# Batch 0's queries, keys and parts inside the self-attention pairs, and pair 7's norm inside the first maxima

## The reference

```
x = layernorm(x + self_attention(x))        # 4 heads, learned windows, q = (x Wq) Wqkv
x = layernorm(x + cross_attention(x, ctx))  # 16 heads of 16 channels
x = layernorm(x + experts(x))               # 8 experts, 2 per token
# cross attention:
Q = x wq + bq;  K = ctx wk + bk;  V = ctx wv + bv
out = softmax(Q K / 4) V, then @ wo + bo
```

## Time and profile before

| | |
|---|---|
| median of 3 runs | 664.44 us (661.35 to 665.6) |
| profiled execution | 663.6 us, its span 661.5 us |
| PE busy | 622.6 us (94%) |
| DVE busy | 373.1 us (56%) |
| ACT busy | 315.1 us (48%) |
| POOL busy | 292.3 us (44%) |

### The profile page before, as it was taken

One profiled execution on the slowest core, in us unless ns is written; L12 is line 12 of the kernel. 1 busy time (PEld: TensorE's weight loads), 2 busy tenths in 40 slices (PEclk: granted clock), 3 DMA queues, 4 the chain that ended last, 5 costly groups with the idle time before them and its releaser, 6 DMA issues.

```text
span 661.5 us, 16872 instructions
## 1 busy us (share of the span) xinstructions
PE 622.6 (94%) x5901; PEld 531.3 (80%) x5902; DVE 373.1 (56%) x996; ACT 315.1 (48%) x813; POOL 292.3 (44%) x526
## 2 busy tenths in 40 slices
PE   6999977999999998999999989999999999999994
PEld 5999954677777776777667768899999999999994
DVE  1778786777777876778767867322222222222245
ACT  2455452777777766777667676121121222112124
POOL 5245365334363349443773342424343342425244
PEclk9999996999999998999989999999999999999998
DMA  8232204565666644444443348688676777666443
GB/s 269 84 93 75 64 28 129 155 193 179 204 191 192 196 135 106 125 119 114 120 107 93 99 140 297 221 274 224 202 211 226 231 231 220 211 195 204 179 138 139
DMA packets 72897, 109.36 MB, mean 165 GB/s; under 512 B 9786, under 2 KB 50562, under 8 KB 72066
## 3 DMA queue, kind: packets, MB, share of 16 engines
q1 hardware_dynamic: 66882, 100.40, 48.7%
q0 software_dynamic: 5952, 8.14, 5.4%
HBM read 73.77 MB, written 12.44 MB: 130 GB/s over the span
## 4 chain that ended last, share of the span: by engine, by line
PE 50%; DMA 19%; issue 10%; DVE 7%; POOLq 6%; POOL 6%; ACT 2%; SPq 0%; DVEq 0%; ACTq 0%
DMA accd<-y,si 18%; PE ps L1603 7%; PE ps L1655 6%; PE ps L1677 6%; PE ps L1630 5%; POOLq L725 5%; PE ps L1614 5%; PE ps L1535 3%; PE ps L1698 2%; PE ps L1663 2%; PE ps L1524 2%; PE ps L1543 2%; PE ps L804 1%; PE ps L1580 1%; POOL r_ln L365 1%
## 5 line engine op out<-in xcount | busy, mean ns | idle before, releaser
L2160 DVE TENSOR_REDUCE cmx<-ps 100x1 f32<-100x361 f32 x256 | 134.6, 531 | 62.9 <-PE ps L1603 58.7
L804 PE MATMUL ps<-xsT,W 128*128 128x128 f32 x1408 | 164.5, 276 | 0.0
L804 PEld LDWEIGHTS ps<-xsT,W 128*128 128x128 f32 x1408 | 160.6, 192 | 0.3
L1930 ACT ACTIVATE cpr<-ps 128x300 f32<-128x300 f32 x256 | 104.8, 419 | 58.2 <-PE ps L1614 57.7
L1603 PE MATMUL ps<-st 96*100 96x361 bf16 x256 | 86.5, 341 | 5.7 <-DVE cmx L2160 4.5
L1614 PEld LDWEIGHTS ps<-st 120*128 120x128 bf16 x768 | 63.2, 102 | 31.9 <-issue 9.3
L853 PE MATMUL ps<-WD,hT 128*128 x384 | 88.1, 380 | 0.5 <-issue 0.5
L1614 PE MATMUL ps<-st 120*128 120x100 bf16 x768 | 77.2, 209 | 3.6 <-ACT st L1935 1.6
L853 PEld LDWEIGHTS ps<-WD,hT 128*128 128x128 f32 x384 | 70.7, 191 | 8.8 <-issue 0.5
L1008 DVE TENSOR_SCALAR y<-ps,wt 128x256 f32<-128x256 f32 x28 | 13.5, 484 | 106.3 <-PE ps L853 106.3
L719 POOL DMA_INDIRECT accd<-y,si x28 | 44.9, 1605 | 64.2 <-DMA accd<-y,si 55.9
(11 more groups left out here) (267 smaller groups left out, 1026.8 us busy)
## 6 DMA issues: line engine op xcount, KB each, us to landing
W<-in_wgu SPq DMA_DIRECT2D x32, 1408.0 KB, 6.5
st<-parts SPq DMA_DIRECT2D x192, 115.2 KB, 2.5
WD<-in_wd SPq DMA_DIRECT2D x6, 1024.0 KB, 5.6
cx<-in_ctxT SPq DMA_DIRECT2D x16, 361.0 KB, 4.5
x_sb<-in_x SPq DMA_DIRECT2D x8, 200.0 KB
x1d<-x SPq DMA_DIRECT2D x8, 200.0 KB
x1Td<-x1T SPq DMA_DIRECT2D x8, 200.0 KB, 3.3
x1T_sb<-x1Td SPq DMA_DIRECT2D x16, 100.0 KB, 3.5
```

Source lines behind the costliest of these rows:

```text
L804: mm = pe.matmul(out[:, i * P:(i + 1) * P], self.columns(t, k, c), self.xsT[:, t.par, k, :], start=(k == 0), stop=(k == KC - 1))
L1930: act.activation(pr[:, h % (2 * HG), :], ps[:, B_T + h % 2, 0:NCH * L], ACT.Exp).then_inc(exp_ok, 1)
L2160: dve.tensor_reduce(mx[:, half, hh:hh + 1], ps[0:L, B_S + h % 2, 0:CTX], AX_X, ALU.max).then_inc(max_ok, 1)
```

## The change

Batch 0's `queries` move to pair 3 and its `keys` to pairs 4 and 5, all in bank 0, the bank of `q_in`; `q_in` of the next pair waits until ScalarE has copied them out. So that x1T_sb is there, `load_x1T(0)` and `(1)` are issued in SyncE's turn g = 2 and no longer in g = 4. Batch 0's parts are made in pairs 4 to 7: `cast` is ScalarE's version of `first_part`, `rest` and `third_part` stand around the masks on VectorE, `copy_first` ahead of `add_bias` on POOL, and the two `stack` calls in SyncE's turns 6 and 7. Batch 1's keys and queries follow pair 7's scores in turn 7, its first parts are casts on ScalarE too. The turnings of pair 7 have nothing in between any more. VectorE runs pair 7's softmax right behind pair 6's norm, and `a_normalise(7)` moves into the turn i = -1, behind maximum 5; `turn_x1` of pairs 6 and 7 go to heads 6 and 12 of that turn. ScalarE computes `window_out(g)` ahead of the second exponential in all pairs from 1 on. Nothing is computed that wasn't.

```diff
+def keys_bank(b, m):
+    return M0 + m if b else B_QIN
 with nc.Block() as block:
...
             load_x(g + 2)
+        if g == PAIRS - 1:
+            stack(0, 1)
         if 2 <= g < PAIRS:
             store_T(g - 2)
-        if g == 4:
+        if g == 2:
             sp.wait_ge(x1T_out[0], 16)
...
             load_x1T(1)
-        if g == PAIRS - 1:
+        if g == PAIRS - 2:
             stack(0, 0)
-            stack(0, 1)
         if 1 <= g < PAIRS:
...
     load_x1T(2)
-    store_T(PAIRS - 2)
     for i in ITER[1:]:
...
             a_store(PAIRS - 1)
+            store_T(PAIRS - 2)
             store_T(PAIRS - 1)
...
     for g in range(1, PAIRS):
+        if PAIRS - 3 <= g < PAIRS - 1:
+            copy_first(0, g - PAIRS + 3)
         add_bias(g)
...
             finish(g - 1)
-    copy_first(0, 0)
     finish(PAIRS - 2)
-    copy_first(0, 1)
     pool.wait_ge(cross_in, 16 * cross.LOADS)
     pool.tensor_copy(bvr[:, :, :], bv_sb[:, :].unsqueeze(2).to_broadcast([P, KC, L])).then_inc(c_step, 1)
+    copy_first(1, 0)
+    copy_first(1, 1)
     finish(PAIRS - 1)
...
             R.below(pool, GROUP_AT[i])
-        if kq:
+        if kq and i >= 0:
             copy_first(i + 2, 0)
...
         wait(pe, dx_ev, g)
+        if g == PAIRS - 4:
+            pe.wait_ge(q_ev, 1)
+        if g > PAIRS - 4:
+            pe.wait_ge(k_ev, min(g - PAIRS + 4, 2))
         for m in range(KC):
...
         for k in range(KC):
-            mm = pe.matmul(ps[:, M0 + m, 0:CTX], wk_sb[:, k, m * P:(m + 1) * P], cx[b % NX][:, k, :],
+            mm = pe.matmul(ps[:, keys_bank(b, m), 0:CTX], wk_sb[:, k, m * P:(m + 1) * P], cx[b % NX][:, k, :],
                            start=(k == 0), stop=(k == KC - 1))
...
             for k in range(KC):
-                mm = pe.matmul(ps[:, M2, m * L:(m + 1) * L], wq_sb[:, k, m * P:(m + 1) * P],
+                mm = pe.matmul(ps[:, M2 if b else B_QIN, m * L:(m + 1) * L], wq_sb[:, k, m * P:(m + 1) * P],
                                x1T_sb[b % 2][:, k, :], start=(k == 0), stop=(k == KC - 1))
...
             pe.wait_ge(consts, 7)
-        if g == PAIRS:
-            pe.wait_ge(k_ev, 1)
-            keys(1, 0)
-        if 1 <= g <= PAIRS:
-            turn_probs(g - 1, 0)
-        if g == PAIRS - 1:
+        if PAIRS - 5 <= g < PAIRS - 2:
+            pe.wait_ge(dx_ev, g + 1)
+        if g == PAIRS - 5:
             pe.wait_ge(cross_in, 16 * cross.LOADS)
-            pe.wait_ge(dx_ev, PAIRS)
+            queries(0)
+        if g == PAIRS - 4:
             keys(0, 0)
-        if g == PAIRS:
-            pe.wait_ge(q_ev, 1)
-            queries(1)
+        if g == PAIRS - 3:
+            keys(0, 1)
         if 1 <= g <= PAIRS:
+            turn_probs(g - 1, 0)
             turn_probs(g - 1, 1)
-        if g == PAIRS:
-            pe.wait_ge(k_ev, 2)
-            keys(1, 1)
         if g + 1 < PAIRS:
...
         if g == PAIRS - 1:
-            pe.wait_ge(qk_ev, 2 * PAIRS)
-            queries(0)
-            keys(0, 1)
-        if 2 <= g <= PAIRS:
+            pe.wait_ge(dx_ev, PAIRS)
+            keys(1, 0)
+        if 2 <= g < PAIRS:
             turn_x1(g - 2)
+        if g == PAIRS - 1:
+            pe.wait_ge(qk_ev, 2 * PAIRS)
+            queries(1)
+            keys(1, 1)
     for i in ITER[1:-1]:
...
                 query_scores(i + 1, h)
-            if h == 8 and i < 0:
+            if h == 6 and i < 0:
+                turn_x1(PAIRS - 2)
+            if h == 12 and i < 0:
                 turn_x1(PAIRS - 1)
...
+    def cast(b, m):
+        act.wait_ge(k_ev, 2 * b + m + 1)
+        act.wait_ge(q_ev, b + 1)
+        wait(act, kq_in[m], 16 * SLOTS * b)
+        act.activation(parts[:, m, 4, :], kf[:, m, :], ACT.Copy).then_inc(k1_ok, 1)
     def second_part(b, m):
...
         qk_out(g, 1)
-        if g == PAIRS - 1:
+        if g >= 1:
             window_out(g)
...
             weff_out()
-        if g < PAIRS - 1:
+        if g == 0:
             window_out(g)
...
             v_out(g)
+        if g == PAIRS - 5:
+            act.wait_ge(cross_in, 16 * cross.LOADS)
+            act.mul(bq4[:, :], bqk_sb[:, 0:KC], 1.0 / np.sqrt(DH)).then_inc(act_set, 1)
+            act.wait_ge(act_set, 2)
+            queries_out(0)
+        if PAIRS - 4 <= g < PAIRS - 2:
+            keys_out(0, g - PAIRS + 4)
         if g >= 1:
...
             relu(g + 1)
+        if PAIRS - 3 <= g < PAIRS - 1:
+            second_part(0, g - PAIRS + 3)
+        if PAIRS - 4 <= g < PAIRS - 2:
+            cast(0, g - PAIRS + 4)
         if 2 <= g < PAIRS - 1:
             x1T_copy(g - 2)
-    act.wait_ge(cross_in, 16 * cross.LOADS)
-    act.mul(bq4[:, :], bqk_sb[:, 0:KC], 1.0 / np.sqrt(DH)).then_inc(act_set, 1)
-    keys_out(0, 0)
-    act.wait_ge(act_set, 2)
-    queries_out(0)
-    keys_out(0, 1)
-    second_part(0, 0)
+    keys_out(1, 0)
     x1T_copy(PAIRS - 3)
     a_exps(PAIRS - 1, 0)
-    second_part(0, 1)
-    keys_out(1, 0)
+    queries_out(1)
     a_exps(PAIRS - 1, 1)
     probs_out(PAIRS - 1, 0)
-    queries_out(1)
-    probs_out(PAIRS - 1, 1)
     keys_out(1, 1)
-    x1T_copy(PAIRS - 2)
+    probs_out(PAIRS - 1, 1)
+    cast(1, 0)
+    cast(1, 1)
+    second_part(1, 0)
+    second_part(1, 1)
     for i in ITER[1:-1]:
...
                 keys_out(i + 2, 1)
-            if h == 10 and i < 0:
-                x1T_copy(PAIRS - 1)
-            if h == 5 and kq:
+            if h in (7, 13) and i < 0:
+                x1T_copy(PAIRS - 2 if h == 7 else PAIRS - 1)
+            if h == 5 and kq and t:
                 second_part(i + 2, 0)
...
             dve.wait_ge(consts, 7)
+        if PAIRS - 3 <= g < PAIRS - 1:
+            rest(0, g - PAIRS + 3)
+        if g == PAIRS - 1:
+            third_part(0, 1)
         masks(g)
+        if g == PAIRS - 2:
+            third_part(0, 0)
         if g >= 1:
             a_normalise(g - 1)
-    first_part(0, 0)
-    rest(0, 0)
-    softmax_in(PAIRS - 1, (0,))
-    first_part(0, 1)
-    rest(0, 1)
-    third_part(0, 0)
-    softmax_in(PAIRS - 1, (1,))
-    third_part(0, 1)
-    a_normalise(PAIRS - 1)
+        if g == PAIRS - 1:
+            softmax_in(g)
     for i in ITER[1:]:
...
                     R.spread_total(dve)
-            if h == 2 and kq:
+            if h < 2 and i < 0:
+                rest(1, h)
+            if 3 <= h < 5 and i < 0:
+                third_part(1, h - 3)
+            if h == 5 and i < 0:
+                a_normalise(PAIRS - 1)
+            if h == 2 and kq and i >= 0:
                 first_part(i + 2, 0)
-            if h == 3 and kq:
+            if h == 3 and kq and i >= 0:
                 rest(i + 2, 0)
```

More of the change, by code:

```diff
@@ L1741, in _ @@
                         pe.wait_ge(consts, 7)
-                    if g == PAIRS:
-                        pe.wait_ge(k_ev, 1)
-                        keys(1, 0)
+                    if PAIRS - 5 <= g < PAIRS - 2:
+                        pe.wait_ge(dx_ev, g + 1)
+                    if g == PAIRS - 5:
+                        pe.wait_ge(cross_in, 16 * cross.LOADS)
+                        queries(0)
+                    if g == PAIRS - 4:
+                        keys(0, 0)
+                    if g == PAIRS - 3:
+                        keys(0, 1)
                     if 1 <= g <= PAIRS:
                         turn_probs(g - 1, 0)
-                    if g == PAIRS - 1:
-                        pe.wait_ge(cross_in, 16 * cross.LOADS)
-                        pe.wait_ge(dx_ev, PAIRS)
-                        keys(0, 0)
-                    if g == PAIRS:
-                        pe.wait_ge(q_ev, 1)
-                        queries(1)
-                    if 1 <= g <= PAIRS:
                         turn_probs(g - 1, 1)
-                    if g == PAIRS:
-                        pe.wait_ge(k_ev, 2)
-                        keys(1, 1)
                     if g + 1 < PAIRS:
@@ L2056, in _ @@
                             attended_out(i - 1)
-                        if h == 9 and kq:
+                        if h == 9 and kq and t:
                             second_part(i + 2, 1)
@@ L2134, in masks, with softmax_in @@
                     mk.then_inc(mask_ok, 1)
-                def softmax_in(g, halves=(0, 1)):
-                    for hp in halves:
+                def softmax_in(g):
+                    for hp in range(2):
                         n = 2 * g + hp
@@ L2303, in _ @@
                             normalise(i - 1)
-                        if h == 6 and kq:
+                        if h == 6 and kq and i >= 0:
                             third_part(i + 2, 0)
-                        if h == 7 and kq:
+                        if h == 7 and kq and i >= 0:
                             first_part(i + 2, 1)
-                        if h == 8 and kq:
+                        if h == 8 and kq and i >= 0:
                             rest(i + 2, 1)
@@ L2313, in _ @@
                             moments(i - 1)
-                        if h == 11 and kq:
```

(1 more changed line is left out.)

8 lines of the change are left out of this document (4 added, 4 removed).

## The result

The changed kernel takes 669.03 us (median of 18 runs, 665.81 to 672.72), the kernel before 664.66 beside it (18 runs, 661.01 to 666.93). The ratio on record is 1.0075 with a 95% interval of [1.0057, 1.0094]: slower, by 4.4 us in the medians (whose quotient is 1.0066) and by 5.0 us by the ratio. The forecast was 670.3.

The account below looks back on a forecast made before the run. TensorE was taken to bound the pairs, with VectorE's chain in the seam. Moved matmuls 3.5, stall 4.8 and half clock 2.3 us, less 4.3 from the seam, gave 6.3 us later: 670.3 us, range 665 to 674.

Parts of the forecast that it names:

- The moved matmuls: Pairs 3 to 5: batch 0's queries and keys lengthen a TensorE without idle time by 3.5 us.
- The wait: Pair 3: TensorE stalls 4.8 us (bounds 1.5 to 5.8) until x1T_sb is stored and loaded back.
- The half clock behind it: After pair 3's stall: 4 to 6 us at half clock, costing 2.3 us (0 to 3.8).
- Sum at pair 7: At pair 7's start: moved matmuls, stall and half clock together make it 10.6 us later.
- Pairs 6 and 7 fit: Pairs 6 and 7: the parts fit into VectorE's idle time at zero cost, pairs again taking 10.1 us.
- The seam: Pair 7's start to first key scores: +36.7 us (35.3 to 38.5) instead of +41.05, giving back 4.3 us.
- To the end, one for one: Batches behind the seam: TensorE is saturated, so a shift at the first key scores passes nearly whole to the end.
- The stall is absent: Rival, pair 3: data is there when TensorE comes, 0.8 us less than before, 662.8 us; chance 0.06.
- Short transfers: Rival, pair 3: store and load take 2.0 us each, stall 1.5 us, 664.3 to 666.6 us; chance 0.08.
- The seam returns little: Rival, seam: half clock for all 16 heads' scores, return only 1.8 us, time 672.5 us; chance 0.14.
- The stall without the clock: Rival, pair 3: the stall comes but the clock holds, 2.3 us less, 668 us; chance 0.10.
- Faster: Rival: no stall, and the first maximum's 9 us gain survives as the norm fits into waits; 658 us, chance 0.04.

Follow-up runs that it names:

- nowait: Changed kernel with batch 0's queries reading a tensor present from the start, so without the wait for x1T_sb; 664.24 us, ratio 1.0006 to the kernel before.
- changed: First profiled trace of the changed kernel itself, nothing further altered; median 669.03 us, ratio 1.0075 to the kernel before.
- after_again: The changed kernel measured and profiled once more, unaltered; 669.64 us.
- norm_first: Changed kernel with pair 7's norm back ahead of batch 0's maxima; 668.89 us, ratio 1.0063 to the kernel before.
- after_fill: Changed kernel with 7 unread matmuls ahead of pair 7's turnings and weighing; ratio 1.0080 to the kernel before.
- after_seam: Changed kernel with unread matmuls ahead of pair 7's turnings and weighing and in the scores' waits for maxima; 663.65 us, ratio 0.9996 to the kernel before.
- filler: Changed kernel with 12 unread matmuls ahead of batch 0's queries in pair 3; ratio 1.0068 against 1.0104 for the changed kernel.
- the rotated ones: Changed kernel with keys in pairs 3 and 4, queries in pair 5; second version also has pair 7's norm ahead; 666.13 and 665.80 us, ratios 1.0017 and 1.0019.
- before_fill: Kernel before with 14 unread matmuls ahead of pair 7's two turnings of the probabilities; 662.06 us, ratio 0.9977 to the kernel before.
- window_alone: Kernel before with only the window's store moved ahead of the second exponential from pair 1 on; ratio 1.0002 to the kernel before.
- store_first: Changed kernel with SyncE issuing batch 0's x1T store ahead of its wait for xb; ratio 1.0067 to the kernel before.

## Why the prediction came out right, and which terms were off

**The moved matmuls**, 3.5 us forecast. nowait against before: 1.2 for the queries (w2 to w3) and 2.75 for both keys (w3 to w6), 3.9 in all. The queries' share holds 0.23 us of waiting for ScalarE's copy, which the forecast took as hidden behind the turnings; each pair with keys takes 1.36 us more, not 1.24.

**The wait**, 4.8 us forecast, 3.26 to 3.36 measured in the five traces that have it in full (changed, after_again, norm_first, after_fill, after_seam). The mechanism was right; the term that was mis-sized is the load, 3.5 us forecast and 2.0 measured, right behind its store as I had noted, in both traces of the change. The store was right (3.9; 3.8 and 3.9). I had seen that the load would stand directly behind the store and kept the 3.5 of a load at 63.1 nonetheless; the minimum of that group of rows was the right value for one of the two transfers. The load at 63.1 was issued 0.4 us behind the issue of another 200 KB store (62.64), the change's load 3.8 us behind that of its store, which had landed. That this made the difference isn't shown. By the Trainium skill's formula (DMA: Bandwidth & Descriptors, Anatomy of one DMA), which that section gives for transfers issued by GpSimd while these are SyncE's, both would take an estimated 4.7 us; measured are 5.8, forecast were 7.4, so the truth lay between the two.

**The half clock behind it**, 2.3 us forecast; 1.3 by filler (up to 1.7 with the tail between w3 and w6 in the changed kernel's trace). A mean clock of 0.90 over 16.47 us is 3.3 us at half, not 4 to 6. The stretch was taken too long, and its cost with it.

**Sum at pair 7**, +10.6 forecast; with the start's spread taken out, w2 to w6 shows 49.60 - 40.49 = 9.1 us, and 8.8 in after_again. The three terms as measured add up to 8.5. Pairs 6 and 7 fit, as said.

**The seam.** I gave back 4.3 us from pair 7's start on; w6 to k gives 43.97 - 37.99 = 6.0, above the 2.5 to 5.8 that I had allowed, and 5.4 in after_again. Head 0's scores stood at +17.8 behind pair 7's projections (88.03; forecast 18.5), the first key scores at +35.1 (forecast 36.7). From w6 to w8 the return is 6.7 in every variant that keeps the change's order of the moved work (5.8 in the rotated ones); from w8 to k the changed kernel loses 0.8 to 1.4 us against before. Half clock there was in the forecast, but I had it as a cost of the norm among the maxima, and norm_first shows it without that norm there (mean clock 0.72 for 0.73). It goes with TensorE's waits in general: the kernel before has it too (0.69 from w8 to k), and before_fill shows that it pays for it. I also had not counted that the full clock ahead of w8 comes with the change; that is 1.5 of the 6.7 us, if before_fill's gain there can be carried over.

**To the end, one for one.** At the first key scores the two traces of the change are 3.1 and 3.4 us late counted from w2, and the times 4.4 us by the medians, 5.0 by the ratio. Between the first key scores and the experts' first product the change takes 279.5 and 278.6 us, the kernel before 277.5, window_alone, which has the code of before in all of it, 278.05, and after_seam 276.2. after_seam has the change's code there, and so have nowait, filler, store_first, norm_first and after_fill, with 277.8 to 279.3. So the same code takes 276.2 to 279.5 us there in one execution or another, and what sets it stays open; "one for one" holds only to within such a spread. It matters for how good the forecast was: at the first key scores I had +6.3 us, and the traces have 3.1 and 3.4. The wait, its clock and the seam were all milder than forecast, by 1.5, 1.0 and 1.1 to 1.7 us, and only the moved matmuls dearer by 0.4. The mechanism was right, but at the first key scores the amount was about twice too large. That the median of 669.03 lies close to 670.3 is in part luck: it contains 1.0 to 1.9 us that these traces do not place ahead of the batches.

**The rivals.** "The stall is absent" was worked out as 0.8 us less than before; nowait, that very case, is 0.06 less at the first key scores and 1.0006 in the median. "Short transfers" was half right: the load took 2.0 us, the store did not. "The seam returns little" did not hold: it returned 6.0 and 5.4. "The stall without the clock" did not hold: the clock fell behind the wait, though it cost 1.3 us and not 2.3. "Faster" did not come even without the stall (nowait).

## What to carry to other kernels

When a matmul moves ahead of its data, price the whole way of the data from the first issue that can send it, and put first what needs no transfer: with the keys in front of the queries the wait of 3.3 us and its half clock were gone, at the same work (1.0075 to 1.0017). And look at the granted clock in every stretch where TensorE waits for another engine in short turns. There, 14 matmuls that nobody reads made the kernel before 0.2% faster (0.9977), and 24 took the change from 1.0075 or 1.0080 to 0.9996, though its trace accounts for only a part of that. Seven in waits where the clock was full already were worth nothing (1.0080). In four traces a gain ahead of that stretch was partly lost in it.
